# A macaron layer (FFN, state-space mixer, FFN): the out-projection's bias and the second FFN's residual move from GpSimd additions to TensorE matmuls into PSUM

## The reference

```python
x = x + 0.5 * ffn(layernorm(x), W1, b1, W2, b2)        # no activation between W1 and W2; 8 groups of 512 tokens
x = x + ssm(layernorm(x), ...)
x = x + 0.5 * ffn(layernorm(x), W1, b1, W2, b2)

def ssm(x):                                            # D_INNER 512, D_STATE 16, DT_RANK 32
    x_in, z = split(x @ Wi.T + bi)
    u  = silu(causal_depthwise_conv4(x_in) + conv_b)
    dt = softplus(x_in[..., :32] @ Wdt.T + bdt)
    h  = h * exp(dt * A) + dt * Bm * u                 # over time, per channel and state
    y  = sum_n(h * Cm)
    return (y * silu(z)) @ Wo.T + bo + x * Dv.mean()
```

## Time and profile before

| | before |
|---|---|
| median of 3 runs | 835.16 us |
| profiled execution, own time | 832.38 us |
| its span, first to last instruction | 830.6 us |
| mean granted TensorE clock | 0.878 |
| DVE busy | 700.6 us (84%) |
| PE busy | 637.5 us (77%) |
| ACT busy | 599.1 us (72%) |
| POOL busy | 281.1 us (34%) |

### The profile page before, as it was taken

One profiled execution on the slowest core, in us unless ns is written; L12 is line 12 of the kernel. 1 busy time (PEld: TensorE's weight loads), 2 busy tenths in 40 slices (PEclk: granted clock), 3 DMA queues, 4 the chain that ended last, 5 costly groups with the idle time before them and its releaser, 6 DMA issues.

```text
span 830.6 us, 8007 instructions
## 1 busy us (share of the span) xinstructions
PE 637.5 (77%) x2794; PEld 318.2 (38%) x2794; DVE 700.6 (84%) x484; ACT 599.1 (72%) x1046; POOL 281.1 (34%) x160
## 2 busy tenths in 40 slices
PE   4875568779987789896997699995746997844947
PEld 4631133434523255543442354632111644210635
DVE  2424764879999999999999998999999999999930
ACT  2465767687995888997687879998776898764432
POOL 0006301030285953242295921259930041100000
PEclk9995779899989899999887999997977998865998
DMA  8230326153447323062628060342324332513001
GB/s 304 100 128 24 114 76 252 51 187 119 179 156 258 119 117 111 4 251 76 255 76 278 1 227 1 126 152 91 138 91 137 138 91 112 167 59 144 1 0 51
DMA packets 39432, 103.05 MB, mean 124 GB/s; under 512 B 4000, under 2 KB 12960, under 8 KB 38880
## 3 DMA queue, kind: packets, MB, share of 16 engines
q1 hardware_dynamic: 36832, 94.40, 31.0%
q10 hardware_dynamic: 2560, 8.14, 4.3%
HBM read 23.08 MB, written 4.19 MB: 33 GB/s over the span
## 4 chain that ended last, share of the span: by engine, by line
PE 23%; DVE 19%; ACT 19%; issue 18%; POOL 6%; DMA 3%; ACTq 1%; DVEq 0%; POOLq 0%
DVE G L1118 17%; ACT G L998 8%; PE MB L1190 6%; PE Y L1264 6%; PE MB L1231 3%; DMA XI<-XI 2%; PE MB L1209 2%; PE MB L1188 2%; ACT XN L824 2%; POOL MS L783 2%; ACT XI L918 2%; POOL LV L744 2%; PE MB L1285 1%; ACT XF L844 1%; ACT L900 1%
## 5 line engine op out<-in xcount | busy, mean ns | idle before, releaser
L998 ACT ACTIVATE G<-RD,COL 128x1024 f32<-128x1024 f32 (+1 forms) x272 | 276.3, 1087 | 107.3 <-PE Y L1264 105.7
L1118 DVE TENSOR_TENSOR_SCAN G<-G,STT,RV 128x1024 f32<-128x1024 f32 (+1 forms) x144 | 319.7, 2277 | 4.8 <-ACT G L998 4.3
L1118 DVE TENSOR_TENSOR_SCAN G<-G,RV 128x1024 f32<-128x1024 f32 (+1 forms) x128 | 276.1, 2215 | 9.3 <-DMA RV<-DW 7.0
L1264 PE MATMUL Y<-G,RW 128*32 128x512 f32 x1024 | 149.8, 707 | 91.5 <-DVE G L1118 76.9
L1264 PEld LDWEIGHTS Y<-G,RW 128*32 128x32 f32 x1024 | 29.6, 121 | 182.5 <-DVE G L1118 99.2
L1231 PE MATMUL MB<-XI,DIAG 128*64 128x512 f32 x248 | 74.6, 737 | 29.4 <-DMA XI<-XI 29.4
L744 POOL TENSOR_TENSOR LV<-LV,HALF 128x4 f32<-128x4 f32 x24 | 42.5, 1772 | 159.9 <-DVE LV L1073 158.4
L736 POOL TENSOR_SCALAR LV<-LV 128x4 f32<-128x4 f32 x18 | 16.3, 908 | 231.7 <-ACT XN L824 231.7
L767 POOL TENSOR_SCALAR X<-X,LV 128x256 f32<-128x256 f32 x32 | 86.6, 2716 | 0.8
L1190 PE MATMUL MB<-MT,XF 128*128 128x256 f32 x256 | 69.5, 410 | 5.9 <-ACT XF L844 5.8
L783 POOL TENSOR_SCALAR MS<-MS,MV 128x256 f32<-128x256 f32 x12 | 36.9, 3082 | 91.1 <-DVE MV L1052 91.1
(11 more groups left out here) (85 smaller groups left out, 742.0 us busy)
## 6 DMA issues: line engine op xcount, KB each, us to landing
RD<-DW SPq DMA_DIRECT2D x60, 512.0 KB, 3.6
RV<-DW SPq DMA_DIRECT2D x60, 512.0 KB, 5.5
W<-in_w SPq DMA_DIRECT2D x48, 256.5 KB, 3.3
XI<-XI ACTq DMA_DIRECT2D x30, 256.5 KB, 5.2
X<-in_x SPq DMA_DIRECT2D x8, 512.0 KB, 5.0
out<-X SPq DMA_DIRECT2D x8, 512.0 KB, 3.0
G<-in_w SPq DMA_DIRECT2D x2, 1026.0 KB, 9.5
RV<-in_w SPq DMA_DIRECT2D x2, 1026.0 KB, 15.1
```

The source lines that it names most:

```text
L998: eng.activation(G[:, i % NG, t0:t1], RD[:, q, t0:t1], ACT.Exp, scale=NAC[:, states(i):states(i) + 1]).then_inc(sems["exp"])
L1118: eng.tensor_tensor_scan(g, g, RV[:, (4 * k + q) % NR, t0:t1], STT[:, idx:idx + 1] if goes_on else 0.0, ALU.mult, ALU.add).then_inc(sems[" ...
L1264: ins = eng.matmul(Y[32 * q:32 * q + 32, 512 * h:512 * h + 512], RW[:, states(i + o), :], G[:, (i + o) % NG, 512 * h:512 * h + 512], start ...
```

## The change

1. `skip` ends after the four one-input instructions; the addition of BO on POOL is gone. For it each `opa` and `opm` has one more matmul of 128x256, identity times BO (in iteration 3 only in the first of the two halves of the projection), and PE waits for BO once.
2. `res` is gone. The second FFN adds its residual by the identity matmul in all iterations, ACT copies the sum from PSUM straight into X, and the store waits for that copy. The XN buffer is free once its transposes are done.
3. Numbers of the table: `outs` starts at scan 2 in place of 1, `back1` at (1, 1) in place of (0, 13), `first1` at (0, 3) in place of (0, 1), `merge1` at (1, 4) in place of (1, 6). The second `repw` transfer is issued behind scan 9 in place of 12.

```diff
-PLAN = {"outs": (0, 1), "back0": (0, 11), "back1": (0, 13), "x0": (0, 0), "first0": (0, 10), "front0": (0, 1),
+PLAN = {"outs": (0, 2), "back0": (0, 11), "back1": (1, 1), "x0": (0, 0), "first0": (0, 10), "front0": (0, 1),
...
-SENDS, LATE = {9: (0,), 12: (1, 2), 14: (3,)}, {14: (0, 1, 2), 15: (3,)}
+SENDS, LATE = {9: (0, 1), 12: (2,), 14: (3,)}, {14: (0, 1, 2), 15: (3,)}
...
 def free(c):
 
-    return ("res", c // 6, c % 2) if c % 6 // 2 == 2 and c < 18 else ("xt", c, 1)
+    return "xt", c, 1
...
         if ph:
-            if it < 3:
-                do("res", it, hf)
             do("store", 2 * it + hf)
...
                     for i in range(4):
                         ins = eng.tensor_scalar(v[:, i, :], v[:, i, :], lv[:, 5, i:i + 1], lv[:, 6, i:i + 1],
                                                 ALU.mult, ALU.subtract)
-                    ins.then_inc(sems["skipv"])
-                    eng.wait_ge(sems["skipv"], count.value["skip", (c,)])
-                    eng.tensor_tensor(v, v, BO[:, :].unsqueeze(1).broadcast_to([P, 4, 256]), ALU.add
-                                      ).then_inc(sems["skip"])
-                elif stage == "res":
-                    it, hf = a
-                    v, xn = X[:, (2 * it + hf) % NX, :, :], tokens(6 * it + 4 + hf)[5]
-                    for pr in range(2):
-                        e.wait_ge("ffn", it, 1, hf, pr)
-                    eng.tensor_tensor(v, v, xn, ALU.add).then_inc(sems["res"])
+                    ins.then_inc(sems["skip"])
...
                     if ph:
-                        dst = v if it == 3 else tokens(6 * it + 4 + hf)[5]
-                        e.wait_ge("xt", 6 * it + 4 + hf, 1)
-                        eng.activation(dst[:, 2 * pr:2 * pr + 2, :].rearrange("p i d -> p (i d)"), bank("fm", *a), ACT.Copy
+                        eng.activation(v[:, 2 * pr:2 * pr + 2, :].rearrange("p i d -> p (i d)"), bank("fm", *a), ACT.Copy
                                        ).then_inc(sems["ffn"])
...
-                        if summed:
-                            eng.matmul(o, ident, v[:, t, :], start=(i == 0), stop=False)
+                        eng.matmul(o, ident, v[:, t, :], start=(i == 0), stop=False)
...
                     eng.matmul(o, ident, v[:, t, :], start=(i == 0), stop=False)
+                    if half == 0 or it < 3:
+                        eng.matmul(o, ident, BO[:, :], start=False, stop=False)
```

More of the change, by code:

```diff
@@ L54 @@
 AT = {unit: i for i, unit in enumerate(UNITS)}
-PLAN = {"outs": (0, 1), "back0": (0, 11), "back1": (0, 13), "x0": (0, 0), "first0": (0, 10), "front0": (0, 1),
-        "x1": (0, 2), "first1": (0, 1), "front1": (0, 10), "ln0": (1, 1), "ln1": (2, 0), "merge0": (2, 5),
-        "merge1": (1, 6), "outs3": (0, 14), "skips": (3, 10)}
+PLAN = {"outs": (0, 2), "back0": (0, 11), "back1": (1, 1), "x0": (0, 0), "first0": (0, 10), "front0": (0, 1),
+        "x1": (0, 2), "first1": (0, 3), "front1": (0, 10), "ln0": (1, 1), "ln1": (2, 0), "merge0": (2, 5),
+        "merge1": (1, 4), "outs3": (0, 14), "skips": (3, 10)}
 DTS, PROJ = -21, -25
-SENDS, LATE = {9: (0,), 12: (1, 2), 14: (3,)}, {14: (0, 1, 2), 15: (3,)}
+SENDS, LATE = {9: (0, 1), 12: (2,), 14: (3,)}, {14: (0, 1, 2), 15: (3,)}
 REST = 4
@@ L605, in build @@
         heads = [G[:, 0:5, :].rearrange("p a n -> p (a n)"), RV[:, 0:5, :].rearrange("p a n -> p (a n)")]
-        sems = {name: ctx.enter_context(nc.semaphore("s_" + name)) for name in [*count.total, "skips", "skipv", "mv1"]}
+        sems = {name: ctx.enter_context(nc.semaphore("s_" + name)) for name in [*count.total, "skips", "mv1"]}
         norms = list(dict.fromkeys(item[0] for stage, item in count.value if stage in ("sum", "vsum", "sq")))
@@ L687, in do @@
                     g, = a
-                    if g < 6:
-                        e.wait_ge("res", g // 2, g % 2)
-                    else:
-                        for pr in range(2):
-                            e.wait_ge("ffn", g // 2, 1, g % 2, pr)
+                    for pr in range(2):
+                        e.wait_ge("ffn", g // 2, 1, g % 2, pr)
                     ov = out[512 * g:512 * g + 512, :].rearrange("(i p) d -> p i d", p=P)
@@ L1179, in do @@
                     v = X[:, g % NX, :, :]
-                    summed = ph == 0 or it == 3
                     claim(e, "fm", *a)
@@ L1186, in do @@
                         o = bank("fm", *a)[:, 256 * i:256 * i + 256]
-                        if summed:
-                            eng.matmul(o, ident, v[:, t, :], start=(i == 0), stop=False)
+                        eng.matmul(o, ident, v[:, t, :], start=(i == 0), stop=False)
                         for j in range(2):
                             ins = eng.matmul(o, XF[:, j, 128 * t:128 * t + 128], MT[:, g % NX, j, :],
-                                             start=(i == 0 and j == 0 and not summed), stop=(i == 1 and j == 1))
+                                             start=False, stop=(i == 1 and j == 1))
                     ins.then_inc(sems["fm"])
@@ L1272, in do @@
                     e.wait_ge("wo")
+                    e.wait_ge("bo")
                     last = 4 * it + 3 if half else 4 * it + 2
```

1 line of the change is left out of this document (removed).

## The result

| | before | after |
|---|---|---|
| median | 835.2 us (835.1 to 835.75, 4 runs) | 814.88 us (812.86 to 815.53, 4 runs) |
| profiled execution, own time | 832.38 us | 815.53 us |
| its span | 830.6 us | 813.7 us |
| mean granted clock | 0.878 | 0.903 |

The ratio is 0.9761, 95% interval 0.9738 to 0.9784. The medians lie 20.3 us apart, the two profiled executions 16.9 us. Measured a second time, the same two kernels gave 815.01 and 833.71 us, ratio 0.977 [0.9742, 0.9798].

The account below looks back on a forecast made before the run. DVE was taken to bound the kernel, with PE close behind at iteration turns. Terms 21.5 + 0.7 - 4.2 = 18.0 us off the 835.2 us median gave 817.2 us, range 811.0 to 826.0.

Parts of the forecast that it names:

- Removed holds, 21.5 and 0.7 us: DVE time saved by removing POOL's additions L771 and L778: 21.5 us between 250 and 712 us, 0.7 in iteration 0.
- the head: Iteration 0, L771 at 88.5: a DVE normalisation takes 1.35 us more; worth between 0 and 1.4, taken as 0.7.
- The rule of the whole lock: Rival: one-input instructions lock too; each of 12 later additions removed is worth 2.34 us, 28.1 in all; 811.3 us, chance 0.08.
- off by one-input instructions: Departure from the skill's rule: beside one-input L767 a scan takes 2.48 us, only 0.2 more than alone.
- The work on PE, 56 x 0.43 = 24.1 us: Added PE work, 32 bias and 24 residual matmuls at 0.43 us each; PE busy near 662 us afterwards.
- Given back, 4.2 us: Time lost where added matmuls delay reductions and exponentials without lead: 2.6, 0.7 and 0.9 us, together 4.2.
- at k5 m2: Out-projection beside k4: three bias matmuls of 0.43 us ahead of a reduction without lead; with k9 m2, 2.6 us.
- at k6 m0 and k10 m0: Second FFN in k5/k6 and k9/k10: four residual matmuls ahead of a reduction, 0.45 us each, 0.9 together, between 0 and 1.5.
- In k13 ... nothing: Second FFN in k13: larger lead, and exponentials of m1 no longer behind the squares, so no cost from residual matmuls.
- Every added matmul is paid: Rival: lead used up everywhere, 24.1 us of PE work against 21.5 gained; 837.8 us, up to 861, chance 0.06.
- PE takes DVE's place: Rival at the turns: half the 56 matmuls precede scans without lead, 12.0 us lost, 9.5 left; 825.7 us, chance 0.12.
- The change does not do what it says: Rival: the next POOL instruction moves into the gap and holds DVE as long; 835 us within 0.2%, chance 0.04.

Follow-up runs that it names:

- the halves: Two runs of the changed kernel: bias back on POOL without its 32 matmuls, 825.47 us; second-FFN residual of iterations 0 to 2 back on POOL without its 24, 823.12 us.
- the next 32: The changed kernel with each of the 32 bias matmuls issued twice, 88 added matmuls in place of 56: 825.02 us, ratio 0.9899.

## Why the prediction was right or wrong, point by point

**The time.** Forecast 817.2 us, range 811.0 to 826.0; measured 814.88, and 815.01 the second time. The forecast gain of 18.0 us lies between the profiles' 16.9 and the medians' 20.3 and 18.7.

**Removed holds, 21.5 and 0.7 us: right.** DVE is busy 22.3 us less with the same instructions; the halves alone gave 12.4 and 9.9 for forecasts of 12.7 (with the whole 1.4 of the head) and 10.2. No scan of 1024 takes more than 2.5 us (nine took more than 2.6 before). Of the head nothing certain reached the end: in the second half pass of k0 the scans are 0.2 us early in one profile and 1.5 in the next, and at k3 m1 all profiles of changed kernels lie between 2.6 early and 0.8 late.

**The rule of the whole lock: wrong in its length, right in its reach.** The Trainium skill (SBUF — State Buffer, Who interferes with whom) has a DVE instruction with two SBUF inputs contend with any GpSimd instruction that reads SBUF, and calls the shared port pair an exclusive lock. The one-input instruction of 1024 held a scan 0.8 us, so it is true that one input suffices. But L767 is 1.22 us long and holds 0.2, so the length is not the measure in its case. My step "off by one-input instructions" stood on this shortest case; the sum did not hang on it, since none of them was removed. With the rule's other half, that DVE in turn shuts GpSimd out, the trace agrees: L739 takes 1.01 us alone and 2.97 or 4.15 among scans, and L767 among scans that follow without a pause often 4.55, about two of their 2.27.

**The work on PE, 56 x 0.43 = 24.1 us: the price right, the forecast of PE's busy time wrong.** The bias matmuls stand on the chain at 0.43 us each:

```profile
485.39 0.63 PE MB L1265 x2
486.02 0.43 PE MB L1267 x2
486.45 1.73 PE MB L1269 x8
```

but PE is busy 648, not 662 us: I had added the work to the old busy time as if the granted clock stayed. It rose from 0.878 to 0.903, and the reductions (L1264 before, L1245 after) went from 149.8 to 141.9 us of busy time. Even beside the same kernel without the matmuls (630.5 and 631.8 us) PE is busy only 16.3 to 17.6 us more.

**Given back, 4.2 us: the size seen in the profiles, its cause only in part, its places partly wrong.** The mechanism, reduction late, exponentials late, scan waiting, is seen at the turns, and DVE's waits for anything but POOL grew by 3.5 to 3.6 us. The single terms are off: at k5 m2 the lead held (0 for 1.3); at k9 the scans wait at m0 and m2 in one profile (1.34 and 1.10, of which 0.56 stood there before, for 1.3), and at m0 not at all in the other; at k6 m0 and k10 m0 the loss is 0 and 0.3 in one profile, and a scan waits 0.7 at k10 m0 in the other (0.9 for both); at k13 m0 0.6 in one profile and 0 in the other (0.7). "In k13 ... nothing" failed: 2.0 and 2.9 us went at k14 m1 and m2, on a chain through the XI transfer that I had not followed. And as a price of the matmuls the term is too large by what the times show: leaving all 56 out brings about 1 us. Of the two profiles without them one has no such wait and the other 3.1 us. So the forecast of the sum owes something to luck: the loss came, about as large as I said, but leaving the matmuls out gives most of it back in some runs and not in others. What takes its place in the others is read only in part, from the POOL instructions.

**The rivals.** "Every added matmul is paid" is refuted for these 56 by the kernels without them, and three quarters true of the next 32. "PE takes DVE's place" did not come, but at 825.0 with 88 added matmuls it stands close by: the cover was thinner than my even lead of 4.7 us suggested. That a late reduction delays the next one too is my reading; no run tests it. The table moves, priced at nothing, are worth 0 to 1.5 us with the old instructions. "The change does not do what it says" is refuted by DVE's busy time, 678.3 us for a forecast of 679; POOL's is 236.4 for 235.

## What to carry to other kernels

Compare the same instruction with and without a neighbour on POOL: a two-input addition of 1024 there costs DVE 2.1 us, though POOL itself is idle two thirds of the time, and splitting it changes nothing. Work moved to an engine that is 77% busy can be nearly free and three quarters of the next half as much paid; test the cover by doubling part of the added work, not only by removing it. Before a loss at one place is put down to a cause, lay every kernel's profile beside it: two of them here contradict what one seemed to show. And when one profile out of several shows a gain of a few us that its median does not, look for an instruction whose length depends on where it falls.

## What the runs showed of the hardware

- The hold of a two-input DVE instruction goes roughly by the elements that POOL reads: 2.1 and 0.5 us for 1024 and 256 with two inputs, 0.8 and 0.2 with one. Only L767, with scalars from SBUF, tells this from a hold by length. The normalisation, with one input of 256 elements and its scalars, is held too: 2.73 us for 1.38 beside L771.
- DVE's scans hold POOL as well: the 128x4 power L739 takes 1.01 us with DVE idle, 2.97 and 4.15 among scans. Part of the scatter between runs of one kernel was traced to it.
- A one-input POOL instruction of 128x256 with scalars from SBUF takes 1.22 us with DVE idle, one of 128x1024 with constants 1.05: time does not go by elements from one form to the other.
- The mean granted clock of the profiled runs was 0.876 to 0.881 in kernels with POOL's additions of both kinds, 0.887 and 0.891 in the changed kernel without the 56 matmuls, 0.901 and 0.903 with them, and 0.904 with 88. Over all runs the step is smaller: 0.894 without them (10 runs, 0.887 to 0.902), 0.899 with them (8 runs, 0.890 to 0.905), 0.900 with 88 (5 runs).
- The second FFN's group in k13 comes after 4.35 us in which PE had nothing to do. The granted clock was 1.00 before, 0.65 and 0.56 in the next 2.1 and 2.2 us, and 1.00 again from 680.2 us on. An identity matmul took 1.06 us at 678.05 and 0.59 at 680.29; in the second profile the first one behind the same pause took 1.19.
